# Value products of two or four groups of heads accumulate in the same output rows, in two attentions with keys on partitions

## The reference

```
# layer 0, cross attention: 16 heads of 8 channels, 120 keys of the context
q = (layernorm(x) @ Wq + bq), k = (ctx @ Wk + bk), v = (ctx @ Wv + bv)     # split in 16 heads of 8
attn = softmax(clip(q k^T * 8**-0.5, -1e4, 1e4))
x = x + tanh(g) * ((attn v, heads side by side) @ Wo + bo)

# layer 1, inside the feed-forward part: 16 heads of 4 channels on a latent of 64, causal
c = rmsnorm(x) @ w_down;  q = rope(c @ wq), k = rope(c @ wk), v = c @ wv    # split in 16 heads of 4
attn = softmax(q k^T / 2, causal)
x = x + (attn v, heads side by side) @ w_up
```

## Time and profile before

| | a_att, 120 to 260 us | dt, 1500 to 1640 us | whole span |
|---|---|---|---|
| TensorE products | 121.35 us busy of 140 | 127.69 us busy of 140 | 1809.2 us, 91% |
| VectorE | 137.24 us | 133.13 us | 1517.5 us, 76% |
| ScalarE | 92.32 us | 95.81 us | 1145.9 us, 58% |
| GpSimd | 99.26 us | 116.96 us | 1167.4 us, 59% |
| TensorE's granted clock | 0.99 | 1.00 | |

### The profile page before, as it was taken

One profiled execution on the slowest core, in us unless ns is written; L12 is line 12 of the kernel. 1 busy time (PEld: TensorE's weight loads), 2 busy tenths in 40 slices (PEclk: granted clock), 3 DMA queues, 4 the chain that ended last, 5 costly groups with the idle time before them and its releaser, 6 DMA issues. The chain is left out here.

```text
span 1992.7 us, 38462 instructions
## 1 busy us (share of the span) xinstructions
PE 1809.2 (91%) x11942; PEld 1353.0 (68%) x11942; DVE 1517.5 (76%) x3061; ACT 1145.9 (58%) x2941; POOL 1167.4 (59%) x1158
## 2 busy tenths in 40 slices
PE   3888886799999999997899999998889998799998
PEld 2455554588888888873777777776545556588886
DVE  5699978677787787767566666765869997677876
ACT  1366645455555555552577777775446666455554
POOL 4777746467676777665233333233788885667764
PEclk9999998799999999999799999999999998799999
DMA  6111100555555565530000000000000000222222
GB/s 126 47 46 46 48 17 14 127 141 135 146 145 143 129 145 145 131 86 9 5 5 5 5 5 4 2 1 1 1 1 1 0 1 17 72 79 64 82 67 69
DMA packets 99648, 115.27 MB, mean 58 GB/s; under 512 B 18064, under 2 KB 55120, under 8 KB 99504
## 3 DMA queue, kind: packets, MB, share of 16 engines
q1 hardware_dynamic: 96576, 112.14, 21.7%
q10 hardware_dynamic: 2928, 1.39, 0.3%
HBM read 101.82 MB, written 3.28 MB: 53 GB/s over the span
## 5 line engine op out<-in xcount | busy, mean ns | idle before, releaser
L76 POOL TENSOR_TENSOR b_moe_hid_low<-b_moe_hid,b_moe_hid_high 128x512 fp32r<-128x512 f32 x256 | 331.7, 1296 | 173.4 <-ACT b_moe_hid_high L1054 171.7
L1060 ACT ACTIVATE bank<-bank 128x512 f32<-128x512 f32 x384 | 223.5, 582 | 333.8 <-PE bank L83 333.8
L1763 POOL TENSOR_TENSOR XC<-XC,c_recip 128x480 f32<-128x480 f32 x128 | 126.8, 990 | 293.4 <-DVE c_recip L1933 293.4
L1085 DVE TENSOR_TENSOR b_moe_gu<-bank,XC 128x512 f32<-128x512 f32 x256 | 176.5, 689 | 116.6 <-PE bank L83 101.9
L76 POOL TENSOR_TENSOR e_moe_hid_low<-e_moe_hid,e_moe_hid_high 128x512 fp32r<-128x512 f32 x128 | 165.6, 1294 | 84.1 <-ACT e_moe_hid_high L1054 83.3
L1887 ACT ACTIVATE XC<-bank,c_shift 128x120 f32<-128x120 f32 x512 | 176.9, 364 | 19.4 <-DVE c_shift L1923 19.4
L71 DVE CAST c_ts_high<-bank 128x480 fp32r<-128x480 f32 x128 | 84.1, 657 | 134.2 <-PE bank L83 133.5
L1090 DVE TENSOR_TENSOR b_moe_hid<-bank,b_moe_gu 128x512 f32<-128x512 f32 x256 | 176.9, 691 | 9.3 <-POOL b_moe_hid_low L76 0.7
L1054 ACT ACTIVATE b_moe_hid_high<-b_moe_hid 128x512 fp32r<-128x512 f32 x256 | 160.0, 625 | 18.7 <-DVE b_moe_hid L1090 18.1
L1882 ACT ACTIVATE c_probT<-bank 120x512 f32<-120x512 f32 x128 | 76.6, 598 | 107.1 <-PE bank L1809 102.4
L1085 DVE TENSOR_TENSOR e_moe_gu<-bank,XC 128x512 f32<-128x512 f32 x128 | 88.3, 690 | 62.1 <-PE bank L83 51.0
(11 more groups left out here) (388 smaller groups left out, 5663.5 us busy)
## 6 DMA issues: line engine op xcount, KB each, us to landing
XC<-b_comb SPq DMA_DIRECT2D x256, 256.0 KB, 4.4
XC<-e_comb SPq DMA_DIRECT2D x64, 256.0 KB, 3.1
X<-in_x SPq DMA_DIRECT2D x4, 512.0 KB, 8.7
a_att_qs_high<-XC SPq DMA_DIRECT2D x32, 64.0 KB, 1.8
a_att_qs_low<-a_Q_low SPq DMA_DIRECT2D x32, 64.0 KB, 1.9
a_att_ks_high<-a_K_high SPq DMA_DIRECT2D x32, 64.0 KB, 1.9
a_att_ks_low<-a_K_low SPq DMA_DIRECT2D x32, 64.0 KB, 1.9
b_moe_w_gate<-in_b_wgT SPq DMA_DIRECT2D x8, 256.0 KB, 2.9
```

The costliest lines, as they stand in the source:

```text
L76: return eng.tensor_tensor(low.bitcast(F32R), x, high, ALU.subtract)
L1060: act.activation(gate_b[j % 4][:], gate_b[j % 4][:], ACT.Silu).then_inc(s_silu, 1)
L1085: dve.tensor_tensor(gu[j % 2][:], up_b[j % 2][:], comb[j // 2][:, (j % 2) // share, :], ALU.mult).then_inc(s_gu, 1)
L1763: pool.tensor_tensor(prob[r % 8], prob[r % 8], recip[:, r % 8, :].unsqueeze(2).broadcast_to([P, HG, NKV]), ALU.mult).then_inc(s_norm, 1)
```

## The change

Two groups of heads (`a_att`) or four (`dt`) now share their 32 output rows and their 128 output columns. The 32 columns of the stationary operand are divided in parts: of 16 columns in `a_att` (8 of values, one of ones), of 8 in `dt` (4 of values, one of ones; the other 4 channels of each head there were zeros before). The values of a group stand in the part that belongs to it, and the other columns are zero. The products of the groups that share rows are accumulated: the first with `start`, the last with `stop`. The number of products and their sizes stay the same. The result fills 256 columns of the bank in `a_att` and 128 in `dt`, in place of 512, and as many are copied, in two transposes and one, in place of four. The heads come out in another order, which the rows of the projection weights (`a_wo`, `d_up8`) follow in the input layout. The values are copied into `vh` by two instructions a round, or four, and the ones are set by four for each buffer.

```diff
+            share, columns = (2, 8) if clamp else (4, 4)
+            pitch = 32 // share
+            outputs = NG // share
-            outs = f32("outs", [P, NG * P])
+            outs = f32("outs", [P, outputs * P])
...
                     for u in range(2):
-                        i = pool.memset(vh[u][:, :, 8:9], 1.0)
+                        for g in range(NG):
+                            one = pitch * (g % share) + columns
+                            i = pool.memset(vh[u][:, HG * g:HG * g + HG, one:one + 1], 1.0)
                     i.then_inc(s_clear, 1)
...
                             wait(pool, s_pv, b - 3)
-                            pool.tensor_copy(vh[u][:, :, 0:8],
-                                             V[:, bass.ds(b * P - 2 * P, P)].rearrange("p (h d) -> p h d", h=H)).then_inc(s_vprep, 1)
+                            values = V[:, bass.ds(b * P - 2 * P, P)].rearrange("p (o s j d) -> p o s j d", o=outputs, s=share, j=HG)
+                            spread = vh[u][:].rearrange("p (o s j) d -> p o s j d", o=outputs, s=share)
+                            for k in range(share):
+                                i = pool.tensor_copy(spread[:, :, k, :, pitch * k:pitch * k + columns],
+                                                     values[:, :, k, :, 0:columns])
+                            i.then_inc(s_vprep, 1)
...
                             pe.wait_ge(s_outs, t - 3)
-                            for g in range(NG):
+                            for g in range(outputs):
                                 i = pe.transpose(out_b[:, g * P:(g + 1) * P], outs[:, g * P:(g + 1) * P], ident[:])
...
                             for g in range(NG):
+                                o = slice(g // share * P, g // share * P + P)
                                 for j in range(HG):
-                                    i = pe.matmul(out_b[32 * j:32 * j + 32, g * P:(g + 1) * P], vh[1 - u][:, HG * g + j, :],
-                                                  probT[1 - u][:, g, j * P:(j + 1) * P], start=True, stop=True)
+                                    i = pe.matmul(out_b[32 * j:32 * j + 32, o], vh[1 - u][:, HG * g + j, :],
+                                                  probT[1 - u][:, g, j * P:(j + 1) * P], start=(g % share == 0),
+                                                  stop=(g % share == share - 1))
...
-                            act.activation(outs[:], out_b[:], ACT.Copy).then_inc(s_outs, 1)
+                            act.activation(outs[:], out_b[:, 0:outputs * P], ACT.Copy).then_inc(s_outs, 1)
...
-                            o = out_b[:].rearrange("p (h c) -> p h c", h=H)
-                            dve.reciprocal(recip[:].unsqueeze(2), o[:, :, 8:9]).then_inc(s_recip, 1)
+                            o = out_b[:, 0:outputs * P].rearrange("p (h c) -> p h c", h=H)
+                            dve.reciprocal(recip[:].unsqueeze(2), o[:, :, columns:columns + 1]).then_inc(s_recip, 1)
...
+    def shared(m, share):
+        m = m.reshape(NG // share, share, HG, 8, -1)
+        return t(m.transpose(0, 2, 1, 3, 4)).reshape(H * 8, -1)
```

More of the change, by code:

```diff
@@ L2297, in layout @@
     w = {
-        "a_wq": n["L0_xattn_Wq"], "a_wk": n["L0_xattn_Wk"], "a_wv": n["L0_xattn_Wv"], "a_wo": n["L0_xattn_Wo"],
+        "a_wq": n["L0_xattn_Wq"], "a_wk": n["L0_xattn_Wk"], "a_wv": n["L0_xattn_Wv"], "a_wo": shared(n["L0_xattn_Wo"], 2),
         "a_bq": n["L0_xattn_bq"].reshape(D, 1), "a_bk": n["L0_xattn_bk"].reshape(D, 1),
@@ L2310, in layout @@
         "d_v": t(np.concatenate([in_eights(n["L1_ffn_wv"])] * 2, axis=0)),
-        "d_up8": up8.reshape(D, D), "d_router": n["L1_ffn_router_w"],
+        "d_up8": shared(up8, 4), "d_router": n["L1_ffn_router_w"],
         "e_wg": t(n["L1_ffn_w1"].transpose(1, 0, 2)).reshape(D, E1 * I1),
```

## The result

The changed kernel took 2001.36 us in the median of nine runs (1996.24 to 2012.6), the kernel before 1993.31 us (1986.97 to 1998.91) in nine runs on the same chip. The ratio is 1.0056, with a 95% interval from 1.0039 to 1.0073: slower by some 11 us. The ratio goes with the means, which are 11.0 us apart; the medians are 8.1 us apart. Forecast were 5.3 us. The sign and the range held, the size didn't: it is twice what was forecast. The sign is that of the sum alone, since the chances beside it leaned a little the other way: 0.47 for a time within 4 us of before, 0.42 for slower.

A forecast was written before the change was run, and what follows sets the result against it. VectorE was taken to pace `a_att`, row maxima then TensorE to bound `dt`. Settled rounds 0, ends -0.9 us, clock +6.2 us gave +5.3 us: 1997.3 us against the median of 1991.97, range 1989.5 to 2004.

The forecast's parts named there:

- the sum: Whole program: 0 for settled rounds, -0.9 us at the ends, +6.2 us for the clock: +5.3 us.
- TensorE's clock: Lean stretches of `a_att`: less work brings four further clock falls at 1.55 us, +6.2 us; no fall in `dt`.
- Transposes: Settled rounds: 0.22 us (`a_att`) and 0.33 us (`dt`) removed inside TensorE's wait for row maxima; worth nothing, uncovered 17.6 us.
- The copy by ScalarE: Each round: fewer columns than 512 give back 0 to 0.6 us of ScalarE's time, worth nothing.
- GpSimd's copies: Each round: one copy becomes two or four, up to +0.29 us (`a_att`) or +0.87 (`dt`), fitting idle time; nothing.
- The ones: Stage starts: eight memsets instead of two, up to 0.7 us; costs nothing, at most 1 us for both stages.
- The value product: Both stages: 32 instructions in 1.08 us as before, no price for accumulating; otherwise 0.5 to 0.8 us a round.
- VectorE: Both stages: reciprocal and product read as many numbers as before at another step; nothing in either direction.
- the faster rival: `a_att`: GpSimd's hold-up of VectorE goes, line 712 takes 0.28 us every round, 6.2 us gained, 1984.9 us; chance 0.09.
- The last rounds: Two rounds at each stage's end: fewer transposes release VectorE sooner, 0.18 us each in `a_att`, 0.27 in `dt`; 0.9 gained.
- The first rival: `a_att`: the clock holds and all that goes was hidden, so not slower, 1991.1 us; chance 0.38.

The follow-up runs named there:

- first and second experiment: Changed kernel with two further unread transposes a round in `a_att`, or two plain products in their place; ratios to the kernel before 0.9999 and 1.0001.
- the first experiment: Changed kernel with two further transposes a round in `a_att`, into columns nothing reads; 1992.74 us, ratio to the kernel before 0.9999.

## Why the forecast had the right sign and half the size

*TensorE's clock* was the right mechanism, and the step that failed, by its number. The prediction took "four" further falls at 1.55 us. The price was about right, or somewhat high (1.3 us by the rounds above, 1.0 to 1.7 by the stages, 1.1 by all executions). The number of falls was too small. The profile has 47.8 - 6.8 = 41.0 us more at 1.2 GHz, twelve lengths of 3.4 us. The other runs have fewer. Over the nine executions the mean granted clock is 0.962, against 0.970 for the kernel before in the later comparisons (in this one only its profiled execution's is known, 0.969). 0.008 of 2000 us, doubled since half the clock is lost, is 32 us, nine lengths of 3.4 us in place of four. At 1.0 to 1.4 us each that is 9 to 13 us; 11 us were measured, with an interval from 8 to 15. The median run alone, with 0.964, has some seven lengths and is 8.1 us slower. This count is over the whole program; in the profile 41 of 53 us are in `a_att`. The runs bear it out: the run of 1996.24 us has a clock of 0.969, that of 2001.21 us 0.963, that of 2012.6 us 0.956.

Where the number came from is the mistake to learn from. I took ten stretches that repeat, all with 1.99 to 2.10 us busy in 3 us, found two falls at 1.89, and read 1.89 as the edge; then I let only four of the ten fall, "since a fall is not tied to the rounds". After the change the clock fell behind stretches of 1.89 to 2.16 us busy (the rows above), so the measure of 3 us that I chose does not separate falling from holding, and nothing in the earlier trace rows said how far the ten that held were from the edge. The lean stretch comes back every second round, so the occasion for a fall is there some 16 times and not ten; with nine further lengths of 3.4 us on average, some seven of them in `a_att` if they divide as in the profile, four was too few. That each of the 16 is an occasion is my argument; no run isolates it. The range held by little: the measured ratio on the median of 1991.97 us is 2003, and nine falls at the price of 1.55 would have given 2005, against an upper end of 2004. The range's upper end, cut at eight falls, would not have held the profiled execution.

*Transposes*, hidden in the wait: right. The wait ahead of the second phase grew from 0.73 to 1.13 us in `dt`. In `a_att` the wait of the weight load for the row maxima grew less than the 0.2 to 0.3 us forecast, from 0.72 to 0.91 us by round to 0.85 to 0.94. Four transposes are free in `a_att` as long as the clock holds (first and second experiment). *The copy by ScalarE*: 0, right; it takes 383 and 277 ns. *GpSimd's copies*: 0, right. Four small ones take 4 x 198 ns in `dt`, 0.50 us more than the one, and the idle time ahead of line 76 fell from 0.91 to 0.63 us. *The ones*: eight memsets take 0.33 us, and the stage starts don't show it. *The value product*: no price for accumulating, 1.08 us for 32 as before. All of that together is what the first experiment shows to cost nothing.

*VectorE*: line 725 still takes 0.28 and 0.6 to 0.8 us in turn, so the faster rival did not come about.

*The last rounds*: half right. In `a_att` the transposes take 0.38 us for two instead of 0.60 for four, and VectorE's wait in the last round is shorter by 0.22 us than the 1.96 us that the same line had before (first row):

```profile
276.38 0.26 DVE L695 RECIPROCAL a_att_recip<-bank 128x16 f32<-128x16 f32 x1 [1.96 <-PE bank L577]
...
290.09 0.38 PE L588 MATMUL bank<-ident,a_att_outs 128*128 128x128 f32 x2
290.51 0.26 DVE L708 RECIPROCAL a_att_recip<-bank 128x16 f32<-128x16 f32 x1 [1.74 <-PE bank L588]
```

In `dt` a fall of the clock stands among its last rounds that was not there before, and I had not looked for one at that place. Window and timeline of the changed kernel, and the first of the two waits before the change:

```profile
1671.20:1674.60 3.40, 3.07 (x35) 0.51 0.00 0
```

```profile
1674.63 0.27 PE L588 MATMUL bank<-ident,dt_outs 128*128 128x128 f32 x1
1674.94 0.26 DVE L708 RECIPROCAL dt_recip<-bank 128x16 f32<-128x16 f32 x1 [2.88 <-PE bank L588]
...
1678.26 0.26 DVE L708 RECIPROCAL dt_recip<-bank 128x16 f32<-128x16 f32 x1 [1.64 <-PE bank L588]
```

```profile
1659.11 0.26 DVE L695 RECIPROCAL dt_recip<-bank 128x16 f32<-128x16 f32 x1 [1.58 <-PE bank L577]
```

With the fall the first wait is 1.3 us longer instead of 0.3 shorter; the second, 1.64, is 0.3 us shorter than the 1.96 before. It recurs: all six profiled kernels with the change in `dt` and without fillers there have the fall and 222.9 us for the stage; two with `dt` as before have none there and 221.9 and 222.0 us. (All eight have one more fall, at the stage's start.) So the ends gave 0.4 us in `a_att` and took 1.0 in `dt`, where 0.9 us in all were to be gained. Where no fall at all stands in `dt`, it takes 220.1 us changed (with two fillers at the end) and 220.7 us as before: the gain is there, about as forecast, when the clock holds. In the settled rounds of `dt` the clock held, as forecast.

The first rival, that the clock holds, had a page behind it. The Trainium skill says, in "TensorE: Matmul & The Clock Gate", Part 4, that a transpose "doesn't count as PE-busy the same way". The runs here differ: taking two transposes a round away brought the falls (1.0057), giving two back ended all but one (0.9999), and two plain products, which are more work, did the same (1.0001). The transposes here are of fp32. The measurement decides.

## What to carry to other kernels

Where TensorE isn't the engine that sets the pace and its clock has fallen at times, work taken from it may not be free to remove. Look at each stage's granted clock; if it has fallen there even once or twice, and the lean stretch repeats every round or two, reckon with many falls once a little work goes. Price that with the rounds that contain a fall, and count by how often the lean stretch recurs. Look at the last rounds of a stage, too. A saving that lies wholly in waits brings nothing by itself; if it is wanted for another reason, a few unread products in the wait can keep the clock, as they did here. They are better left out of the last rounds, where they delayed VectorE.

## What the runs showed of the hardware that I had not expected

- 0.22 us less of a 5.7 us round for TensorE (two 128 x 128 transposes) took the granted clock of the stage from 0.99 to 0.87 in the profiled executions, and to 0.96 in that of the kernel before with two transposes.
- Busy time in the 3 us ahead doesn't tell a fall: it fell behind 2.16 us and held behind 1.99. What does, these runs leave open.
- At 1.2 GHz the value product takes 1.94 us instead of 1.08, while the whole stage loses only 0.3 to 0.5 us for each us at half clock, since VectorE sets its pace.
- GpSimd's copy of 16 columns takes 198 ns, of 64 columns 236 ns and of 128 columns 290 ns: by these, about 185 ns of each (an estimate) don't depend on its size.
